# Degree counts from ids split into 5 and 7 bits, and attention programs written out without loops

## The reference, cut to what matters

```python
# layer 0 (attention, both directions of every edge, 4 heads)
idx = jnp.concatenate([edge_index, edge_index[:, ::-1]], axis=0)
src, dst = (idx[:, 0], idx[:, 1])
score = (att * leaky_relu(ngl[src] + ngr[dst], 0.2)).sum(-1)
ex = jnp.exp(score - segment_max(score, src)[src])
alpha = ex / (segment_sum(ex, src)[src] + 1e-16)
out = segment_sum(ngr[dst] * alpha[:, :, None], src)
...
# layer 1: the degree of each node divides the sums over its edges
deg = segment_sum(ones, dst)
inv_deg = (1.0 / jnp.maximum(deg, 1.0))[:, None]
nbr_r = segment_sum(h_r, dst) * inv_deg
...
# layer 3 (attention, 8 heads, self loops)
e = leaky_relu(a_src[src] + a_dst[dst], 0.2)
e = jnp.exp(e - segment_max(e, dst)[dst])
alpha = e / (segment_sum(e, dst)[dst] + 1e-16)
out = segment_sum(alpha[:, :, None] * h[src], dst)
```

## Time and profile before

| quantity | value |
|---|---|
| three runs | 6140.91, 6148.54, 6149.28 us |
| profiled execution | 6139.35 us, of which the span is 6137.6 us |
| GpSimd (POOL) busy | 3783.2 us, 62% |
| VectorE (DVE) busy | 4092.7 us, 67% |
| TensorE (PE) busy | 2661.9 us, 43% |
| ScalarE (ACT) busy | 1253.9 us, 20% |

### The profile page before, as it was taken

The page is one execution under the profiler, slowest core; times in us unless marked ns, Lnnn a source line. Parts: engine busy times, 40 slices in busy tenths (PEclk is TensorE's granted clock), DMA queues, the critical chain, the costliest instruction groups (busy, mean ns, idle before and its releaser), DMA issues.

```text
span 6137.6 us, 56339 instructions
## 1 busy us (share of the span) xinstructions
PE 2661.9 (43%) x13332; PEld 1809.3 (29%) x13333; DVE 4092.7 (67%) x6865; ACT 1253.9 (20%) x4370; POOL 3783.2 (62%) x3760
## 2 busy tenths in 40 slices
PE   1785101011332322222222342677674577777746
PEld 0661101011322222222222242546453232332315
DVE  9778888886986776767676774232322576676655
ACT  0000000000111111111111110000000677777741
POOL 2777777776777777777777774000002777777730
PEclk6555555555555555555555555767685788888876
DMA  6221121211222222222222231435261222332230
GB/s 229 53 54 51 48 56 48 73 29 50 77 79 61 72 61 71 63 70 64 69 64 68 66 85 39 144 104 179 69 205 22 58 83 77 87 86 77 84 98 7
DMA packets 388365, 472.44 MB, mean 77 GB/s; under 512 B 212478, under 2 KB 248384, under 8 KB 381041
## 3 DMA queue, kind: packets, MB, share of 16 engines
q1 hardware_dynamic: 132624, 279.73, 13.8%
q0 software_dynamic: 114832, 129.82, 9.7%
q10 hardware_dynamic: 140752, 61.28, 3.5%
HBM read 291.34 MB, written 179.19 MB: 77 GB/s over the span
## 4 chain that ended last, share of the span: by engine, by line
POOL 58%; issue 21%; PE 9%; DMA 6%; DVE 5%; ACT 0%; POOLq 0%; DVEq 0%; ACTq 0%; SPq 0%
POOL arena L738 44%; POOL rec_dram L695 11%; PE acc L1959 4%; DMA oh<-mt_dram 2%; PE acc L1780 2%; DMA V<-in_edge_attr_dram 2%; DMA rec_dram<-V,rowst 1%; PE acc L1782 1%; PE acc L1943 1%; POOL own_dram L715 1%; POOL pdum L688 1%; POOL arena L765 1%; DVE arena L1579 1%; PE pt L1770 0%; POOL own_dram L769 0%
## 5 line engine op out<-in xcount | busy, mean ns | idle before, releaser
L738 POOL DMA_INDIRECT arena<-tab_dram,jst x2592 | 2685.8, 1036 | 778.3 <-issue 777.8
L695 POOL DMA_INDIRECT rec_dram<-V,rowst x784 | 866.1, 1105 | 229.9 <-issue 217.8
L688 POOL TENSOR_TENSOR pdum<-pdum 128x1 f32<-128x1 f32 x197 | 58.5, 297 | 1138.3 <-DVE arena L1607 864.6
L1902 PE MATMUL pw<-OHX 128*128 128x128 bf16 x1632 | 210.3, 310 | 1120.8 <-DVE OHX L1414 1120.8
L1902 PEld LDWEIGHTS pw<-OHX 128*128 128x128 bf16 x1632 | 156.9, 140 | 1172.3 <-DVE OHX L1414 859.7
L1910 PE MATMUL acc<-arena,oh 128*128 128x64 f32 x1952 | 427.1, 420 | 20.9 <-DVE oh L1423 20.7
L1910 PEld LDWEIGHTS acc<-arena,oh 128*128 128x128 f32 x1952 | 417.2, 330 | 34.9 <-issue 34.9
L900 ACT ACTIVATE arena<-arena,ew 128x64 f32<-128x64 f32 x1728 | 417.8, 333 | 33.3 <-PE acc L1983 33.3
L1437 DVE TENSOR_TENSOR arena<-arena,pt 128x1024 f32<-128x1024 f32 x108 | 131.8, 1221 | 431.7 <-DMA arena<-tab_dram,jst 429.4
L900 ACT ACTIVATE OHX<-arena,ew 128x64 f32<-128x64 f32 x1728 | 417.7, 333 | 2.5
L1983 PE MATMUL acc<-OHX,ident 128*128 128x512 f32 x432 | 253.7, 753 | 371.0 <-ACT OHX L900 371.0
(11 more groups left out here) (523 smaller groups left out, 6463.2 us busy)
## 6 DMA issues: line engine op xcount, KB each, us to landing
oh<-mt_dram SPq DMA_DIRECT2D x90, 512.0 KB, 3.6
arena<-tab_dram,jst POOLq DMA_INDIRECT x2592, 2.5
arena<-rec_dram SPq DMA_DIRECT2D x122, 288.0 KB, 3.6
mt_dram<-oh ACTq DMA_DIRECT2D x272, 128.0 KB, 1.7
oh<-mt_dram SPq DMA_DIRECT2D x75, 416.0 KB, 3.9
oh<-mt_dram SPq DMA_DIRECT2D x75, 384.0 KB, 4.0
rows_dram<-V SPq DMA_DIRECT2D x27, 1056.0 KB, 4.0
rows_dram<-arena SPq DMA_DIRECT2D x27, 1056.0 KB, 4.3
```

What stands on the lines that cost most here:

```text
L695: gp.indirect_dma_start(rec[:, :], bass.IndirectOffsetOnAxis(ap=rowst[:, q, k:k + 1], axis=0), recst[:, q, k, :], None).then_inc(S[f"scat{ ...
L738: gp.indirect_dma_start(hd.G[:, a.r, j, :], None, table[:, :], row_of(jst[:, a.r, j:j + 1])).then_inc(S[f"{x}g{a.r}"], 16)
L1902: last = nc.tensor.matmul(unit_bank(c.slot)[:, k // 2 * P:(k // 2 + 1) * P], mones[c.slot][:, 0, k, :], mones[c.slot][:, 1, k, :], start=k ...
```

## The change

Three edits.

1. Degree counts. An id is split into its 5 low bits (DL = 32 values) and the rest, chunk times four plus two bits (DH = 100 values). The split is made with integer shift and and, and copies to `hi2` and `lo2`; places past the last edge get 127.0, which matches nothing. A step has two compares in place of six: one of 2 x 14 x 100 elements, one of 2 x 14 x 32. TensorE has 28 matmuls a step in place of 42, 14 with 100 columns and 14 with 64 x 200. Afterwards eight small copies put the counts into the old layout, and the 25 x 25 table comes from a reduce and one more matmul.
2. First attention: VectorE's and ScalarE's programs are written out for all 54 blocks (`first_attention_flat`). TensorE, GpSimd and SyncE keep their loops.
3. Last attention: VectorE's program is written out for all 27 blocks (`flat_blocks`). The other engines keep their loops.

```diff
--- before.py
+++ after.py
@@ -76,7 +76,7 @@
 GROUPS, ADDS = NBS + OVB * BT // 4, NC + OVB * BT // 4
 TURNS = (NBS + OVB) // 4
 KP = 14
-NCW = NC + NC % 2
+DL, DH = 32, 4 * NC
 UAT = (0, 5, 10, 15, 20)
 UL = (0, 6, 11, 16, 22, 27, 32)
 ULR = (0, 4, 9, 13, 18, 22, 26)
@@ -157,7 +157,7 @@
         pos = [cols(12), cols(13)]
         sone = cols(14)
         low_i = cols(15, I)
-        lo2, bk2 = [[cols(k + l).bitcast(BF).rearrange("p (j e) -> p j e", e=2) for l in range(2)] for k in (8, 10)]
+        lo2, hi2 = [arena[0:EP, k * EC:(k + 2) * EC].bitcast(BF).rearrange("p (j l e) -> p j l e", l=2, e=2) for k in (8, 10)]
         iota_i = arena2[:, 2 * NG:2 * NG + P].bitcast(I)
         gmat = arena2[0:NC, 0:NG]
         rowidx = arena2[0:EP, 512:512 + EC].bitcast(U)
@@ -191,9 +191,9 @@
         OHX = sb("OHX", [P, 16384], BF)
         OHXf = OHX[:].bitcast(F)
         RG = arena2[:, 0:4 * GT * REC].rearrange("p (r t f) -> p r t f", r=4, t=GT)
-        dgo = OHX[0:EP, 1024:1024 + 4 * KP * (NCW + P)].rearrange("p (q f) -> p q f", q=2)
-        dhi = dgo[:, :, 0:2 * KP * NCW].rearrange("p q (l k n) -> p q l k n", l=2, n=NCW)
-        dlo = dgo[:, :, 2 * KP * NCW:2 * KP * (NCW + P)].rearrange("p q (l k n) -> p q l k n", l=2, n=P)
+        dgo = OHX[0:EP, 1024:1024 + 4 * KP * (DL + DH)].rearrange("p (q f) -> p q f", q=2)
+        dlo = dgo[:, :, 0:2 * KP * DL].rearrange("p q (k x) -> p q k x", k=KP)
+        dhi = dgo[:, :, 2 * KP * DL:2 * KP * (DL + DH)].rearrange("p q (k x) -> p q k x", k=KP)
         t128 = OHXf[0:NC, 512:512 + EP]
         jst = sb("jst", [P, 4, MW], U)
         jsf = jst[:].rearrange("p r x -> p (r x)").bitcast(F).rearrange("p (r x) -> p r x", x=MW)
@@ -443,6 +443,18 @@
             for t in range(LAST, NB0):
                 body(Group(t // 4, t % 4))
 
+        def first_attention_flat(eng, body):
+
+            for t in range(NB0):
+                body(Group(t // 4, t % 4))
+
+        def flat_blocks(n, step):
+
+            step(Group(0, 0), None)
+            for t in range(1, n):
+                step(Group(t // 4, t % 4), Group((t - 1) // 4, (t - 1) % 4))
+            step(None, Group((n - 1) // 4, (n - 1) % 4))
+
         class Steps:
 
             def __init__(self, eng, which, per, g):
@@ -872,7 +884,7 @@
                 after(act, S[f"awr{a.q}"], a.turn2 * 16)
                 A.copy(SO0[:, a.q, :, D + H0:], RUNS[:, a.q, 0:H0 * RB].rearrange("p (h f) -> p f h", f=RB)).then_inc(S["aso"], 1)
                 A.copy(SO0[:, a.q, :, 0:D + H0], ST0[:, a.q].rearrange("p (x f) -> p f x", f=RB)).then_inc(S["aso"], 1)
-            first_attention(act, weights0)
+            first_attention_flat(act, weights0)
             exponentials("a", [CX0[1], CX0[2], FC0, FX0])
             transposed(2 * D)
             ff_up(0, ACT.Gelu, D, b1c0)
@@ -1035,25 +1047,23 @@
                 return iotab[0:parts, 0:wide].rearrange("p (n e) -> p n e", e=2).unsqueeze(1).to_broadcast([parts, tiles, wide // 2, 2])
 
             for l in range(2):
-                for o, values in ((lo2[l], lof[l]), (bk2[l], bkf[l])):
-                    link(V.tensor_copy(o, values.unsqueeze(2).to_broadcast([EP, EC, 2])))
+                link(V.tensor_copy(key_i[0], idf[l]))
+                link(V.tensor_scalar(key_i[1], key_i[0], 5, None, ALU.logical_shift_right))
+                link(V.tensor_scalar(key_i[0], key_i[0], DL - 1, None, ALU.bitwise_and))
+                link(V.tensor_copy(hi2[:, :, l], key_i[1].unsqueeze(2).to_broadcast([EP, EC, 2])))
+                link(V.tensor_copy(lo2[:, :, l], key_i[0].unsqueeze(2).to_broadcast([EP, EC, 2])))
+                for a, e, c in ((0, EX, EF + 1), (EX, 2 * EX, EF), (2 * EX, P, EF)):
+                    link(V.memset(hi2[a:e, c:EC, l], 127.0))
 
             def degree_ones(i, q):
 
                 after(v, S["dgm"], i * 2 + q - 1)
-                part = [0]
-
-                def ones_of(o, values, wide, a, n):
-
-                    k = bass.ds((i * 2 + q) * KP + a, n)
-                    V.tensor_tensor(paired(o[:, a:a + n]), iota_pairs(n, wide, EP),
-                                    values[:, k, :].unsqueeze(2).to_broadcast([EP, n, wide // 2, 2]), ALU.is_equal).then_inc(S["dg"], 1)
-                    part[0] += 1
-                    v.wait_ge(S["dg"], i * 12 + q * 6 + part[0])
-                for l in range(2):
-                    ones_of(dhi[:, q, l], bk2[l], NCW, 0, KP)
-                    ones_of(dlo[:, q, l], lo2[l], P, 0, KP // 2)
-                    ones_of(dlo[:, q, l], lo2[l], P, KP // 2, KP // 2)
+                k = bass.ds((i * 2 + q) * KP, KP)
+                for part, (o, values, wide) in enumerate(((dhi, hi2, DH), (dlo, lo2, DL))):
+                    V.tensor_tensor(paired(o[:, q].rearrange("p k (l n) -> p (k l) n", l=2)), iota_pairs(2 * KP, wide, EP),
+                                    values[:, k].rearrange("p j l e -> p (j l) e").unsqueeze(2).to_broadcast([EP, 2 * KP, wide // 2, 2]),
+                                    ALU.is_equal).then_inc(S["dg"], 1)
+                    v.wait_ge(S["dg"], i * 4 + q * 2 + part + 1)
             pairs(v, EC // (2 * KP), degree_ones)
             v.wait_ge(S["pix"], 2)
             link(V.tensor_copy(kcol[:], pidx_i[:, 7:8]))
@@ -1070,8 +1080,15 @@
             rowi = lcol[:, 200:250].bitcast(I)
             quo, rest = lcol[:, 250:300], lcol[:, 300:350]
             kn = lcol[:, 350:350 + NC]
-            link(V.tensor_copy(degf[:, 0:NC], accw[:, 0:NC]))
-            link(V.tensor_copy(degf[:, NC:2 * NC], pt[:, 0:NC]))
+            for l in range(2):
+                for m in range(4):
+                    link(V.tensor_copy(degf[m * DL:(m + 1) * DL, l * NC:(l + 1) * NC],
+                                       accw[l * DL:(l + 1) * DL, l * DH:(l + 1) * DH].rearrange("p (c m) -> p c m", m=4)[:, :, m]))
+            fours, four_i, four_of = lcol[:, 550:550 + NC], lcol[:, 600:601], lcol[:, 601:602]
+            link(V.tensor_reduce(fours[0:DH], pu[0:DH, 160:160 + DH].rearrange("p (c m) -> p c m", m=4), AX, ALU.add))
+            link(V.tensor_scalar(four_i.bitcast(I), pidx_i[:, 7:8], 2, None, ALU.logical_shift_right))
+            link(V.tensor_copy(four_of, four_i.bitcast(I)))
+            link(V.tensor_scalar(lcol[:, 625:625 + NC], iota[:, 0:NC], four_of, None, ALU.is_equal))
             link(V.tensor_copy(deg[:], degf[:, 0:NC]))
             link(V.tensor_scalar(rowf, degf, float(RK - 1), None, ALU.add))
             link(V.tensor_copy(rowi, rowf))
@@ -1119,7 +1136,7 @@
             row_index(rst_u, rowf, float(2 * P * RP), float(P * RP), 1.0)
             v.wait_ge(S["rst"], 1)
             row_index(rend_u, cumf, float(2 * P * RP + 2 * P), float(P * RP + P), 0.0)
-            count = pu[0:NC, 160:160 + NC]
+            count = acc[0:NC, 512:512 + NC]
             cn, incl, more, mincl, ids, begin, thr, goal, wg, wi, tot, pre = cw
             ci = pads[:, 0:NC].bitcast(I)
             row = lambda u: u[:, 0:NC]
@@ -1467,7 +1484,7 @@
                 V.tensor_tensor_scan(ST0[:, a.q], DX0[:, a.q], RS0, 0.0, ALU.mult, ALU.add).then_inc(S["asc"], 1)
                 v.wait_ge(S["asc"], a.g + 1)
                 assert st.k == 25, st.k
-            first_attention(v, block0)
+            first_attention_flat(v, block0)
             v.wait_ge(S["rmm"], NG)
             link(V.tensor_copy(nbr_r[:], acc_n))
             link(V.tensor_scalar(invdeg[:], deg[:], 1.0, None, ALU.max))
@@ -1673,7 +1690,7 @@
                         weighted3(a, pair, st)
                 assert not a or st.k == 22, st.k
                 assert not c or sums.k == 24
-            blocks(v, NB3, block3)
+            flat_blocks(NB3, block3)
 
             v.wait_ge(S["dtl"], 16)
             link(V.tensor_copy(MR3.rearrange("p (h d) -> p h d", h=H3), TL3[:, 520:528].unsqueeze(2).to_broadcast([P, H3, D])))
@@ -1823,17 +1840,17 @@
 
             def degree_count(i, q):
 
-                pe.wait_ge(S["dg"], 12 * i + 6 * q + 6)
+                pe.wait_ge(S["dg"], 4 * i + 2 * q + 2)
                 for k in range(KP):
                     st_ = isinstance(i, int) and i == 0 and q == 0 and k == 0
-                    nc.tensor.matmul(pu[0:NC, 160:160 + NC], dhi[:, q, 0, k, 0:NC], dhi[:, q, 1, k, 0:NC], start=st_, stop=True, skip_group_check=True)
-                    nc.tensor.matmul(accw[:, 0:NC], dlo[:, q, 0, k, :], dhi[:, q, 0, k, 0:NC], start=st_, stop=True, skip_group_check=True)
-                    last = nc.tensor.matmul(pt[:, 0:NC], dlo[:, q, 1, k, :], dhi[:, q, 1, k, 0:NC], start=st_, stop=True, skip_group_check=True)
+                    nc.tensor.matmul(pu[0:DH, 160:160 + DH], dhi[:, q, k, 0:DH], dhi[:, q, k, DH:2 * DH], start=st_, stop=True, skip_group_check=True)
+                    last = nc.tensor.matmul(accw[0:2 * DL, 0:2 * DH], dlo[:, q, k], dhi[:, q, k], start=st_, stop=True, skip_group_check=True)
                 last.then_inc(S["dgm"], 1)
             pairs(pe, EC // (2 * KP), degree_count)
```

(1 more changed line is left out.)

## The result

The changed kernel takes 6330.4 us (median of 4 runs, 6327.5 to 6338.0) against 6146.0 for the kernel before (6140.9 to 6149.3). The ratio is 1.0303, 95% interval 1.0290 to 1.0316. The sign was forecast, the size was not: 6172 us was forecast, 6128 to 6204 the range.

The account below looks back on a forecast made before the run. GpSimd's indirect gathers and scatters were taken as the bound, with VectorE only altering their length. First attention -36, last attention +41, degree counts +21, extra hits +1 made +27 us on 6144.5: 6172 us, range 6128 to 6204.

Parts of the forecast that it names:

- First attention, -36: VectorE's blocks 4 to 47 written out: smaller gaps hold GpSimd's gathers less, 0.8 us a block, -36 us.
- the sum: Whole kernel: -36 first attention, +41 last attention, +21 degree counts, +1 for hits by added VectorE work: +27 us.
- Last attention, +41: VectorE's blocks 4 to 23 written out: L1643 starts ahead of gathers and holds them, +2.04 us a block, +41 us.
- The first rival: Last attention: gathers escape being held since other engines keep loops; -15 or -46 us in all, 6099 to 6130; chance 0.16.
- the hits: Last attention: three gathers a block start behind VectorE's L1643 and are held, taking 1.8 to 2.0 us.
- Degree counts, +21: Degree stage: shortened to 155 us, 50 us of scatter loss against 28 before, less 1 for phase slips: +21 us.
- the step 2.0, under VectorE's 2.8: Degree stage: TensorE's step takes 2.0 us at 2.4 GHz (up to 4.2 at 1.2), so VectorE's 2.8 sets the pace.
- the high level: Degree stage: TensorE's clock is granted 2.4 GHz, as dense bf16 matmuls elsewhere ran at a granted 0.97.
- The second rival: Degree stage: TensorE stays at 1.2 GHz, +39 there, +45 in all, 6190 us; chance 0.17, shared with a smaller first-attention gain.
- VectorE finishes 85 us earlier, but waits at the key gather anyway: After the degree stage: VectorE's earlier finish was given no gain in the forecast.
- called hidden: After the degree stage: conversions, count copies and count matmul add some 8 us of VectorE, hidden behind scatters, priced +1 us.
- A wait of GpSimd in front of a hold: Listed sign that the forecast is wrong: GpSimd waiting before a hold, which its terms don't include; no size given.

Follow-up runs that it names:

- both wide: Changed kernel with 128 columns of weights in both degree matmuls instead of 100 and 64: 6174.5 us, ratio 1.0046 to the kernel before.
- one wide: Changed kernel with only the 64-column degree matmul widened to 128 columns of weights, the 100 kept: 6179.1 us, ratio 1.0050 to the kernel before.
- 65 columns: Changed kernel with 65 columns of weights in place of 64, the 100 kept: 6178.6 us, ratio 1.0054 to the kernel before.
- grouped: Changed kernel with each step's 14 degree matmuls of 100 columns first, then the 14 of 64: 6179.8 us, ratio 1.0051 to the kernel before.
- the two attentions alone: Kernel before with the three written-out programs (VectorE's two, ScalarE's one) and the old degree counts: 6149.7 us, ratio 1.0006.

## Why the prediction was wrong

- **First attention, -36: right, mechanism and size.** -36.9 by the landmarks, 0.83 us a block against the 0.8 of the sum (44 x 0.8 is 35, which changes nothing).
- **Last attention, +41: right, mechanism and size.** +43.9, and 42 us between two kernels that differ in it alone. The first rival, that the hits would not form while the other engines keep their loops, did not happen.
- **Degree counts, +21: wrong, +179.** VectorE's side of the stage was right (155 us and 85 scatters once TensorE is out of the way); the net +24 holds two terms that the sum lacks, some +14 at the scatters and -13 at the gathers behind them, and they happen to cancel. The step that failed is TensorE's price and the bound that follows from it: "the step 2.0, under VectorE's 2.8", or up to 4.2 at the lower level, taken from the earlier trace rows. Both rows there are runs of matmuls of one shape. The changed stage alternates 64 and 100 columns of weights, and a pair measured 0.555 us, a step 7.8. Of that the columns are 0.25 a pair; the alternation is the other 0.305, and with it gone the pair is 0.25 at the same clock level and 0.13 at the higher one. So TensorE bound the stage, at 7.8 us a step, and not VectorE at 2.8.
- **The clock.** I took the high level because the stream would be dense. It was denser than I thought, without a gap, and stayed at 0.50. It was granted 0.94 to 0.96 in each of the four kernels in which alternation was removed (both wide, one wide, 65 columns, grouped), and 0.50 where it was kept, with the 100 widened too. Why the alternating stream was granted less is not shown. Nor is the clock the main part: without alternation a pair at 0.50 is 0.25 us, a step 3.5, and the stage 196 us (an estimate), shorter than the old 245. The second rival had the right clock, and at +39 was still far off, since it too had no alternation in it.
- **The wait.** "VectorE finishes 85 us earlier, but waits at the key gather anyway" was argued in one direction only. VectorE finished the stage 186 us later (617 instead of 431). It then stood 8.5 us for the last matmuls and made the copies of the counts, which the prediction had called hidden, and SyncE sent the key table off 197 us later. SyncE's row before, then after:

```profile
1436.95 0.33 SPq L584 DMA_DIRECT2D keys_dram<-oh  x1
```

```profile
1633.63 0.33 SPq L596 DMA_DIRECT2D keys_dram<-oh  x1
```

With 2.7 us to landing, the table had been there 17 us before GpSimd came for it at 1456.87 in the kernel before; GpSimd itself came 13 us later in the changed kernel. 197 - 17 - 13 = 167, the wait that was measured. I had not priced what it costs when the cover of 17 us is gone. "A wait of GpSimd in front of a hold" was on the prediction's list of what would prove it wrong, and it is what came.
- **The sign.** Slower was forecast and slower it is, but not for the forecast reason: the two attentions alone measured no change (6149.7 us), and 166 of the 184 us are a wait that the sum doesn't have.
- **The hint was there.** The degree stage of the kernel before already alternates 25 and 128 columns. Its triple takes 0.29 us: by the starts above 0.13 from the 25 to the first 128, 0.05 between the two 128, 0.11 back. With 0.02 us of columns in each, the two changes of width take 0.20. Put on top of the new pair's 0.25, that is 0.45 us a pair, 6.3 a step and 353 us for the stage, 82 less than the measured 435: an estimate near 6250 us, outside the range and on the right side. The earlier trace rows had the stage's clock of 0.50 too. The rows of the very stage were to be had, and I took those of others instead.

That the 0.20 of the kernel before is the same cost as the 0.305 of the changed one is inferred; no run removed it from the kernel before. Weight loads that 25 moved columns are too short to cover would be another reason, and no run excludes it.

## What to carry to other kernels

Price an engine's new instructions from rows of the same mixture in the same stage, not from a uniform run elsewhere, and ask of every engine that the edit touches what happens if it becomes the bound. Where matmuls with 64 columns of weights alternate with wider ones, group them or widen the 64 by a junk column (fewer than 64 were not tried). Even then the degree edit cost 24 us here, since the engine that it relieves wasn't the bound. Where GpSimd's indirect DMAs set the pace, look at the moment at which VectorE's long instructions with two SBUF inputs start against them: a tenth of a microsecond decided over 1 us here.

## What the runs showed of the hardware that I had not expected

- Alternating 64 with 100 columns of weights costs 0.305 us a pair at 1.2 GHz (0.555 for 0.25 us of columns); 65 with 100 in alternation takes 0.25 us a pair at that level. At the higher level 64 in a row take 0.099 us each, and 65 with 100 in alternation 0.13 us a pair.
- A TensorE that shows as busy for 113.9 of 114 us was granted 0.50 throughout, and 0.95 with the same matmuls in another order.
- Five one-element memsets a block in the first attention and eight in the last one, put ahead of long VectorE instructions, took 3% off a kernel that VectorE doesn't bound.
